# A graph network on one core: node rows expanded in destination order and scattered into source order, and each window of edges gathered once

## What is computed

```python
def spmm(h):                       # first layer, used twice
    msg = h[src] * edge_w[:, None] # edge_w = dinv[src] * dinv[dst] * (src != dst)
    return segment_sum(msg, dst) + self_w[:, None] * h

q, k, v = (x @ w.T + b for each)   # second layer: attention over edges, 8 heads of 16
scores = (q[row] * k[col]).sum(per head) / 4 + edge_emb @ eb_w.T + eb_b   # row = src, col = dst
attn = softmax of scores over the edges of equal row
out = segment_sum(attn * v[col], row) @ out_w.T + out_b
```

## Time and profile before

| what | us |
|---|---|
| median of 3 runs | 10343.97 (10342.14 to 10344.8) |
| span of the profiled execution | 10313.9 |
| TensorE matmul busy | 6267.6 (61%) |
| VectorE busy | 6220.2 (60%) |
| ScalarE busy | 2345.7 (23%) |
| GpSimd busy | 7254.5 (70%) |
| DRAM traffic | 852.87 MB, mean 83 GB/s |

### The profile page before, as it was taken

One profiled execution on the slowest core, in us unless ns is written; L12 is line 12 of the kernel. 1 busy time (PEld: TensorE's weight loads), 2 busy tenths in 40 slices (PEclk: granted clock), 3 DMA queues, 4 the chain that ended last, 5 costly groups with the idle time before them and its releaser, 6 DMA issues. The chain is left out here.

```text
span 10313.9 us, 189711 instructions
## 1 busy us (share of the span) xinstructions
PE 6267.6 (61%) x32657; PEld 5084.3 (49%) x32658; DVE 6220.2 (60%) x25485; ACT 2345.7 (23%) x7601; POOL 7254.5 (70%) x8109
## 2 busy tenths in 40 slices
PE   7767777776666666666666666544545445434774
PEld 5544444444555555555555555523444444423664
DVE  8755555554666666666666666654444444458777
ACT  7522222221211111111111111110000000014885
POOL 4577777777677777777777777766777777723665
PEclk9855555555666666666666666655555555557997
DMA  2122222222221221221212212135555555542553
GB/s 81 30 53 53 53 53 52 53 52 53 68 53 53 54 54 52 54 54 52 55 53 53 55 52 54 47 100 178 158 157 156 158 158 158 157 55 81 149 148 99
DMA packets 625544, 852.87 MB, mean 83 GB/s; under 512 B 149806, under 2 KB 429374, under 8 KB 624992
## 3 DMA queue, kind: packets, MB, share of 16 engines
q0 software_dynamic: 241872, 461.43, 17.7%
q1 hardware_dynamic: 383088, 389.29, 13.0%
q10 hardware_dynamic: 544, 1.72, 0.0%
HBM read 683.27 MB, written 168.68 MB: 83 GB/s over the span
## 5 line engine op out<-in xcount | busy, mean ns | idle before, releaser
L1163 POOL DMA_INDIRECT spmm_fetched_rows<-h_table,spmm_index_ring x3330 | 3153.6, 947 | 1019.4 <-issue 1007.2
L1229 PE MATMUL bank<-spmm_fetched_rows,spmm_hot 128*128 128x128 f32 x6660 | 2259.0, 438 | 1931.8 <-DMA spmm_fetched_rows<-h_table,spmm_index_ring 1448.7
L1229 PEld LDWEIGHTS bank<-spmm_fetched_rows,spmm_hot 128*128 128x128 f32 x6660 | 1531.5, 286 | 2536.6 <-issue 1640.5
L1207 DVE TENSOR_TENSOR region_b<-region_b,bank 128x128 f32 x3330 | 956.5, 287 | 2061.6 <-PE bank L1229 2035.7
L1502 POOL DMA_INDIRECT score_kv_rows<-kv_table,score_index_ring x1680 | 1589.0, 946 | 572.4 <-issue 495.4
L632 POOL DMA_INDIRECT s_slots<-spmm_beside_payload,spmm_beside_where x1568 | 1546.7, 986 | 478.5 <-issue 460.0
L1527 PE MATMUL bank<-region_b,score_hot_t 128*128 x3360 | 865.8, 439 | 1080.4 <-DVE score_hot_t L1543 1080.4
L1527 PEld LDWEIGHTS bank<-region_b,score_hot_t 128*128 128x128 f32 x3360 | 744.9, 326 | 1189.4 <-issue 1189.4
L621 ACT COPY spmm_beside_next_slot<-bank 98x128 f32<-98x128 f32 x1568 | 416.2, 265 | 2918.6 <-PE bank L582 2869.4
L1189 DVE TENSOR_SCALAR spmm_hot<-iota_bf,lo_slots 128x128 f32<-128x128 bf16 x3334 | 944.5, 283 | 20.7 <-PE bank L1229 13.1
L587 PE MATMUL bank<-spmm_beside_next_slot,spmm_beside_hi_t 98*128 98x128 f32 x3136 | 945.2, 394 | 0.0
(11 more groups left out here) (308 smaller groups left out, 11544.8 us busy)
## 6 DMA issues: line engine op xcount, KB each, us to landing
v_sorted<-score_kv_rows SPq DMA_DIRECT2D x210, 512.0 KB
mix_v_rows<-v_sorted SPq DMA_DIRECT2D x420, 256.0 KB, 3.0
spmm_beside_attr_sb<-in_edge_attr_dram SPq DMA_DIRECT2D x196, 384.0 KB
spmm_fetched_rows<-h_table,spmm_index_ring POOLq DMA_INDIRECT x3330
score_kv_rows<-kv_table,score_index_ring POOLq DMA_INDIRECT x1680
s_slots<-spmm_beside_payload,spmm_beside_where POOLq DMA_INDIRECT x1568
spmm_beside_attr_sb<-in_edge_attr_dram SPq DMA_DIRECT2D x196, 124.0 KB
h_table<-region_b SPq DMA_DIRECT2D x28, 448.0 KB, 3.0
```

What stands on the lines that cost most here:

```text
L1163: nc.gpsimd.indirect_dma_start(fetched_rows[:, k, :], None, table, bass.IndirectOffsetOnAxis(ap=index_ring[:, k:k + 1], axis=0)).then_inc( ...
L1207: nc.vector.tensor_tensor(here, here, sum_bank[k % 2][:, 0:D], ALU.add).then_inc(added, 1)
L1229: nc.tensor.matmul(sum_bank[k % 2][:, 0:D], hot[:, k % HOTS, :], fetched_rows[:, k, :], start=True, stop=True).then_inc(summed, 1)
```

## The change

Sources, keys and products:
- The source of each edge is held in window order in SBUF (`from_i`), and a product gathers each of the 1568 windows once into a ring of 16. TensorE takes the place of a tile's window in the ring and the number of windows that must have arrived from registers (two loads of 8 values for each 8 tiles). SyncE counts the arrivals, loads the indices of each half by DMA, and GpSimd waits for the tiles that used the windows (`pairs_done`, two values a turn).
- Beside product 1 run `Count` and the bias work (`CountAndBias`). ScalarE's queue loads the attributes, two DMAs a half, and stores the biases to `bias_tab`.
- Beside product 2 runs `RankBySource`: the slot of each edge is found, and kept in SBUF (`where`), with no scatter and no attributes. The two masks of a column come in another way: for two columns at once TensorE turns the one-hots (`turn_pair`), ScalarE copies them twice (`keep_turns`), TensorE compares (`compare_pair`) and ScalarE applies a ReLU (`keep_earlier`). SyncE fills the slots that hold no edge: 112 tiles of 128 rows of 1088 bytes in one DMA at the start, and one tile a turn.

A new stage, `expand`, between the q, k, v stage and scoring: k and v of all nodes stay in SBUF (`kv_nodes`). In destination order a one-hot matmul makes the k and v rows of 128 slots, VectorE adds them into a ring of 16 windows, ScalarE puts place and bias beside them, and GpSimd scatters 128 rows of 1088 bytes (k, biases, place, v) for each window into `kv_sorted`.

The q, k, v stage stores q (64 KB a node tile) instead of k and v (128 KB). Scoring brings q back into SBUF, has no gathers, and reads k, biases and places in order; mixing reads v from the same table (pieces of 512 bytes). `sort_destinations` stands ahead of `window_slots`; it is skipped as before. `find_bases` makes the windows, places and counts.

The core of the diff:

```diff
-    kv_table = dram("kv_table", (NT * P, 2 * D))
+    q_table = dram("q_table", (NT * P, D))
-    v_sorted = dram("v_sorted", (P, S_TILES, D))
+    kv_sorted = dram("kv_sorted", (P * S_TILES, ROW))
...
+        class Ranks:
+            RING = 8
+            LEAD = 4
...
+            def turn_pair(self, pe, u, c, k):
+                pe.wait_ge(self.hot_ready, c + 2)
+                need(pe, self.turns_kept, 2 * u)
+                for m in range(2):
+                    last = nc.tensor.matmul(self.turned_bank[0:NT, m * P:(m + 1) * P], self.hot_hi[:, (k + m) % self.RING, :], ident_bf[:, :],
+                                            start=True, stop=True)
+                last.then_inc(self.turned, 1)
+            def compare_pair(self, pe, u, b):
+                pe.wait_ge(self.turns_kept, 2 * u + 2)
+                need(pe, self.earlier_ready, u)
+                nc.tensor.matmul(self.alike[:, 0:2 * P], ident_bf[:, :], not_before[:, :, :].rearrange("p a b -> p (a b)"), start=True, stop=False,
+                                 skip_group_check=True)
+                for m in range(2):
+                    one = self.hi_t_bf[:, b, m * P:(m + 1) * P]
+                    last = nc.tensor.matmul(self.alike[:, m * P:(m + 1) * P], one, one, start=False, stop=True, skip_group_check=True)
+                last.then_inc(self.alike_ready, 1)
...
+            def tensor_step(self, pe, i, k):
+                if k % 2 == 0:
+                    self.compare_pair(pe, u + 1, (k // 2 + 1) % 2)
...
+            def tensor_end_step(self, pe, i, k):
+                if k % 2 == 1:
+                    self.turn_pair(pe, i * (TURN // 2) + k // 2 + 2, i * TURN + k + 3, k + 3)
+            def keep_turns(self, act, u, b):
+                act.wait_ge(self.turned, u + 1)
+                need(act, self.found, 2 * u - 2)
+                nc.scalar.copy(self.hi_t_bf[:, b, :], self.turned_bank[0:NT, 0:2 * P]).then_inc(self.turns_kept, 1)
+                nc.scalar.copy(self.hi_t[:, b, :], self.turned_bank[0:NT, 0:2 * P]).then_inc(self.turns_kept, 1)
...
+            def scalar_step(self, act, i, k):
+                act.wait_ge(self.counted, c + 1)
+                need(act, self.found, c - 1)
+                nc.scalar.copy(self.next_slot[:, k % 2, :], self.running[0:NT, 0:P]).then_inc(self.next_ready, 1)
+                if k % 2 == 0:
+                    self.keep_earlier(act, u + 1, 1 - b)
+                else:
+                    self.keep_turns(act, u + 2, b)
...
+            def fill_start(self, sp):
+                some = S_TILES - E_COLS
+                sp.dma_start(kv_tiles[:, E_COLS:S_TILES, :], self.blank[:, :].unsqueeze(1).to_broadcast([P, some, ROW])).then_inc(self.tail_filled, 16)
...
+                        work.fill(sp, i)
+                        for h in range(2):
+                            for k in range(h * HALF, (h + 1) * HALF):
+                                sp.wait_ge(fetched[k], i * 16 + 16)
+                                sp.sem_inc(arrived, 1)
+                            if not last:
+                                load_index(i + 1, h)
...
+                            if k % HALF == 0:
+                                some = bass.ds(t, HALF)
+                                place = loaded(mybir.EngineType.PE, window_place[:, some], HALF, TURN, WINDOW_SLOT)
+                                until = loaded(mybir.EngineType.PE, until_window[:, some], HALF, E_COLS, CLAMPED, least=1)
...
-                            pe.wait_ge(fetched[k], (fetched_before(nth, k) + i + 1) * 16)
-                            nc.tensor.matmul(sum_bank[k % 2][:, 0:D], hot[:, k % HOTS, :], fetched_rows[:, k, :],
+                            pe.wait_ge(arrived, until[k % HALF])
+                            nc.tensor.matmul(sum_bank[k % 2][:, 0:D], hot[:, k % HOTS, :], tile_of(rows, place[k % HALF]),
...
+                        pool.wait_ge(extras, (2 * i + h + 1) * 3)
+                        pool.wait_ge(joined, pairs[h])
+                        pool.sem_inc(go, 1)
+                        for k in range(HALF):
+                            nc.gpsimd.indirect_dma_start(kv_sorted, bass.IndirectOffsetOnAxis(ap=where_ring[:, h, k:k + 1], axis=0),
+                                                         payload[:, h * HALF + k, 0:ROW], None).then_inc(scattered[h * HALF + k], 16)
...
+                            v.scalar_tensor_tensor(here, here, same_window[:, bass.ds(t, 1)], made_here, ALU.mult, ALU.add).then_inc(joined, 1)
...
+                        sp.dma_start(k_rows[:, j, :, :], kv_tiles[:, bass.ds(i * TURN + j * GROUP, GROUP), 0:PART]).then_inc(k_in[j], 16)
```

More of the change, by code:

```diff
@@ L48 @@
 CLAMPED = "node tiles are clamped to the last one where the table is built"
+WINDOW_SLOT = "a window's place in a ring, or the place behind it"
 assert N_CHUNKS * CHUNK == NT and N_CHUNKS % 2 == 0 and NT % 2 == 0
-assert 0 < LAST_TILES <= HALF
+assert 0 < LAST_TILES <= HALF and NT == E_TURNS
 assert W_BLOCKS * WINDOWS == S_TILES and CHUNK_TILES * CHUNKS == S_TILES and LAST_COLS % TURN == 0
+assert SRC_BLOCKS * SRC_WINDOWS == E_COLS
 FULL_TURNS = LAST_COLS // TURN
```

1025 lines of the change are left out of this document (635 added, 390 removed).

## The result

The changed kernel takes **10860.52 us** (median of 4 runs, 10856.87 to 10863.31) against 10343.06 (4 runs) for the kernel before: ratio 1.0502, 95% interval 1.0487 to 1.0517. It is 5% slower, where 2% faster was forecast; rival C (10690 to 10895, chance 0.38) is what came, 10 us outside the range. That the time lies within C's two numbers is in part luck: C's own sum for a slow product 2 is 10690, its 10895 wanted the low clock in product 1 too, which did not come (0.62), and 271 us that C does not have are scoring's.

The account below looks back on a forecast made before the run. GpSimd's issue of indirect transfers was taken to bound both products and scoring. Small stages 1219, product 1 2095, product 2 3065, expansion 2020, scoring 960, mixing 750 and 30 around gave 10140 us; range 9500 to 10850.

Parts of the forecast that it names:

- rival C: Product 2 at the low clock nearly throughout, 2.0 to 2.2 us a column: 10690 to 10895 us; chance 0.38.
- The expansion: New stage: GpSimd paces it with 1568 scatters at 1.28 us, 2020 us; bounds 1960 and 2330.
- product 1: First product stage: 1568 columns at 1.26 us plus 119, 2095 us; GpSimd idle for less than 5%.
- mixing: Mixing stage: reads 512-byte pieces instead of 2 KB ones, 750 us, at most 780.
- the small stages: All outside the large stages: changes sum to nothing, 10 us added for one more stage, 1219 us.
- Product 2, the chain: TensorE waits for ScalarE's copies once per pair; 4.33 us a pair at the low clock, 3.01 at the full one.
- Product 2, the clock: Half of product 2's columns at each clock: 1.85 us a column, 2901 us of the stage's 3065.
- rival B: Product 2 at the full clock throughout, 2517 us instead of 3065: 9590 us in all; chance 0.12.
- Product 2, the register loads: TensorE's loads of 16 values per 8 tiles add 0.03 to 0.08 us a column; bounds 0 and 0.26.
- Scoring: Scoring stage: 420 groups at 2.22 us plus 28 to bring q back, 960 us; bounds 930 and 1100.
- The start of product 2: Filling 112 tiles on SyncE's queue ahead of turn 1's index loads adds 35 us.
- A: The forecast itself: mixed clock in product 2, 1.75 to 1.97 us a column, 9980 to 10320 us; chance 0.42.

Follow-up runs that it names:

- e7: The changed kernel with four matmuls that nothing reads put behind the turning of each pair in product 2: 10191 us.
- e5: The changed kernel with turning and comparison taken apart, the comparison later, same work in another order: 9652 us, 0.935 of the kernel before.
- u1: The changed kernel with product 2's two masks made by VectorE from spread keys again, without turning or comparison: 10272 us.
- x3: e5 with two more register loads of eight values per eight columns of product 2 on TensorE, each read by a met wait: 10127 us.
- s1: The changed kernel with a ring of eight groups instead of four in scoring: 10722 us, scoring at 1033 us.
- c0: The changed kernel itself, unedited, run again on a chip where the kernel before took 10322 us: 10850.88 us.
- e1: The changed kernel with the comparison waiting for only the first of ScalarE's two copies, on a chip with stops: 13402 us.

## Why the prediction was wrong

**The expansion; product 1; mixing; the small stages.** Right: within 7, 23, 19 and 34 us. The expansion was priced by a scatter of 40-byte rows (1.28) and came at that pitch with 1088-byte ones, with TensorE's clock at 0.81. In product 1 GpSimd waited 173 us for row products, 8% of the stage, where the prediction's sign was less than 5%.

**Product 2, the chain.** Right in place and size: one wait per pair, released by ScalarE's second copy, 749 us in 784 times. The pair at the low clock was 4.33 without loads and is 4.2 in its typical case, the column with all 2.19 (2.17 without the wait for the fill) against 2.2; at the full clock 3.2 (e7) against 3.01.

**Product 2, the clock: the step that failed.** "... so neither end is excluded, and I take half of the columns at each". The clock was 0.50 throughout, which makes 1568 x (2.2 - 1.85) = 549 us more than the forecast; the stage missed by 478, as its other terms came out a little lower. The mean clock of the stage before (0.66) was taken as a guide, though the change had put a gap of about 1 us (0.95 in the mean) into every pair. e7 shows that these gaps matter: with unread matmuls in them and nothing else changed, 0.94; e5, which takes the gaps out by order alone, has 0.83. What the clock follows in general stays open: u1 has no such gap and stayed at 0.50. (The Trainium skill, TensorE: Matmul & The Clock Gate, Part 1, says that activity releases the throttle: e7 agrees, 0.50 to 0.94. Its other half, that an idle stretch brings the throttle back, gave rival B. The runs bear it out in part at most: product 2 never reached the full clock although the gaps of its pairs were at most 1.7 us, and in e5 from 2760 to 4950 us the clock fell 120 times with no gap of TensorE over 1.95 us.)

**Product 2, the register loads.** Taken at 0.03 to 0.08 us a column with the words that TensorE's sequencer runs ahead. For the changed kernel the number was right: three pairs in four take 4.2, those with loads 4.5 to 4.9 and 4.75 in the mean, so 0.07 a column. The reason was not: the pair's gap hides most of it. Where no gap hides them they stop TensorE for 1.5 us per eight columns, 0.19 a column (e5, u1; x3 for the doubling), not far from the upper bound of 0.26.

**Scoring, the second step that failed.** The 2.22 us per group came from the earlier trace rows, a stretch with rows already there and TensorE at the full clock. Both conditions fail here: with the loads issued only when the group four before is scored, their 3.0 us stands in a chain over three groups, and at a clock of 0.71 the q product takes over 1.8 us, up to 2.07, in half of the groups instead of 1.15. s1 took away the first and half of the second together, for 154 us against c0 and 163 against the first profile. s1 still has 1033/420 = 2.46. The prediction named the late loads, but only as an upper bound, up to 1100, and measured it by bandwidth (133 GB/s), not by latency.

**The start of product 2.** 35 us for the fill: 37.3 measured on GpSimd.

**The chances.** C was given 0.38 and A 0.42; the range ended at C's 10850 while the text had C reach 10895, so the range was cut through the case that came. Had scoring met its 960, the total would have been 10590 and inside the range, with the clock as wrong as it is.

## What to carry to other kernels

Before moving work from a slack engine to a bound one through a third, draw each engine's order for one turn: if TensorE asks for a copy and the next thing in its order needs that copy, the whole latency is a gap, and it costs twice when the clock stays at 1.2 GHz as well, as it did here. Asking one pair earlier (e5) turned a loss of 5% into a gain of 6.5% with the same work. Size a ring by the latency from the release of a place to the landing of its refill, counted in groups, and not by bandwidth alone.

## What the runs showed of the hardware that was not expected

- Adding four unread matmuls to each pair (by estimate 0.4 us at the full clock and 0.8 at the low one, from the 0.11 and 0.21 us that one takes to the next start) made the kernel 660 us faster: they do no part of the work, and the granted clock rose from 0.50 to 0.94.
- Neither the gaps nor the busy share of a stage order its clock here. Product 1 of the changed kernel was granted 0.62 with TensorE busy for 90% and 12 gaps over 1 us in the 1940 us from 560 to 2500. u1 and e5 both have one stop of about 1.5 us per eight columns and no other gap of that size, and are at 0.50 and 0.83, busy for 86 and 82%.
- A register load of eight values takes TensorE 0.59 us, one of four values 0.33; two of eight with what stands around them stop it for 1.3 to 1.7 us.
- One chip ran large loops 6 to 10 us slower per turn (product 1: 3144 instead of 2116 us, expansion: 2648 instead of 1999) and short loops at the usual speed (scoring 1180 us). In product 1 of e1 TensorE and VectorE stood still about every 17 us, twice a turn; their cause is open.
